# A two-hop graph kernel: the tail look-up turned round, and one operand of the second hop's vector operations kept in PSUM

## The reference

```python
def _agg(ent, rel, head, tail, etype, fc_w, fc_b):
    a_input = concatenate([ent[head], ent[tail]], -1)
    e = leaky_relu(sum((a_input @ fc_w.T + fc_b) * rel[etype], -1), 0.2)
    exp_e = exp(e - segment_max(e, head)[head])
    alpha = exp_e / segment_sum(exp_e, head)[head]
    return segment_sum(ent[tail] * alpha[:, None], head) + ent
for _ in range(2):
    ent = _agg(...)
    ent = ent / maximum(norm(ent), 1e-12)
return layernorm(x + ent)
```

## Time and profile before

| | us |
|---|---|
| median of 3 runs | 2868.09 (2825.28 to 2874.2) |
| profiled execution, its own time | 2870.03 |
| its span, first to last instruction | 2867.7 |
| busy: PE / DVE / ACT / POOL | 1218.3 / 1848.4 / 866.2 / 1805.7 |

### The profile page before, as it was taken

One profiled execution on the slowest core, in us unless ns is written; L12 is line 12 of the kernel. 1 busy time (PEld: TensorE's weight loads), 2 busy tenths in 40 slices (PEclk: granted clock), 3 DMA queues, 4 the chain that ended last, 5 costly groups with the idle time before them and its releaser, 6 DMA issues. The chain is left out here.

```text
span 2867.7 us, 22941 instructions
## 1 busy us (share of the span) xinstructions
PE 1218.3 (42%) x4597; PEld 818.2 (29%) x4597; DVE 1848.4 (64%) x3677; ACT 866.2 (30%) x1585; POOL 1805.7 (63%) x1607
## 2 busy tenths in 40 slices
PE   4688801354423544245433534444344345343300
PEld 4577701122211222123212423232223223222200
DVE  6867864286562865546655559877667667766753
ACT  2232304375453754445631212111111111111111
POOL 1000047377774777757777238877777787777776
PEclk9555555555555555555555556665655555566555
DMA  2333333254432444335433133222222222222210
GB/s 68 89 109 103 104 70 84 52 147 131 126 91 71 130 132 131 86 95 150 122 87 114 51 112 89 82 85 79 61 83 87 72 66 84 86 58 66 60 44 13
DMA packets 91815, 255.95 MB, mean 89 GB/s; under 512 B 31782, under 2 KB 39047, under 8 KB 91771
## 3 DMA queue, kind: packets, MB, share of 16 engines
q1 hardware_dynamic: 41403, 183.66, 20.8%
q0 software_dynamic: 50368, 71.78, 11.4%
HBM read 157.76 MB, written 102.23 MB: 91 GB/s over the span
## 5 line engine op out<-in xcount | busy, mean ns | idle before, releaser
L572 POOL DMA_INDIRECT area<-rows,gi x1176 | 1330.2, 1131 | 487.4 <-issue 367.7
L620 POOL DMA_INDIRECT out<-area,place x392 | 459.3, 1172 | 119.5 <-issue 119.5
L765 PE MATMUL psR<-area,row_t 128*98 128x512 f16 (+1 forms) x896 | 302.7, 504 | 454.3 <-DVE area L1191 335.9
L748 PE MATMUL psR<-area 128*128 128x392 f16 x392 | 198.5, 506 | 445.2 <-issue 406.3
L670 PE MATMUL psP<-V,vT 65*125 65x40 f32 (+1 forms) x1586 | 323.4, 393 | 86.1 <-issue 56.6
L670 PEld LDWEIGHTS psP<-V,vT 65*125 65x125 f32 (+1 forms) x1586 | 316.0, 310 | 104.7 <-issue 62.4
L765 PEld LDWEIGHTS psR<-area,row_t 128*98 128x98 f16 x896 | 141.5, 173 | 610.4 <-DVE area L1191 351.9
L908 ACT ACTIVATE area<-area 128x896 f32<-128x896 f32 x84 | 79.8, 950 | 586.2 <-DVE area L1270 433.6
L872 ACT ACTIVATE area<-iota_h,half_hi 128x392 f16<-128x392 f16 x392 | 238.9, 609 | 16.8 <-issue 15.4
L1269 DVE TENSOR_TENSOR area<-SM,rd 128x896 f32<-128x896 f32 x56 | 93.6, 1671 | 206.6 <-DMA out<-area,place 205.4
L774 PE MATMUL psT<-ones,area 98*128 98x1 f32 x700 | 152.6, 352 | 173.5 <-DVE area L1191 131.1
(11 more groups left out here) (269 smaller groups left out, 2296.4 us busy)
## 6 DMA issues: line engine op xcount, KB each, us to landing
rows<-area SPq DMA_DIRECT2D x50, 787.5 KB
area<-tail_digits SPq DMA_DIRECT2D x28, 896.0 KB
rows<-area SPq DMA_DIRECT2D x28, 735.0 KB
area<-rows SPq DMA_DIRECT2D x28, 735.0 KB
area<-rows SPq DMA_DIRECT2D x25, 787.5 KB
area<-rows,gi POOLq DMA_INDIRECT x1176
head_xs<-area SPq DMA_DIRECT2D x28, 448.0 KB
area<-head_xs SPq DMA_DIRECT2D x28, 448.0 KB
```

The lines of the kernel that those rows point to most:

```text
L572: pool.indirect_dma_start(out=to[:, b, k, 0:tab.shape[1]], out_offset=None, in_=tab, in_offset=bass.IndirectOffsetOnAxis(ap=gi[:, b, n, k: ...
L620: pool.indirect_dma_start(out=out, out_offset=bass.IndirectOffsetOnAxis(ap=place[:, b, k:k + 1].bitcast(U32), axis=0), in_=rowO[:, b, k, 0 ...
L748: te.matmul(psC, sign_lo[:, (s0 + k) % KS, :], sign_hi[:, (s0 + k) % KS, :], start=static and t0 + k == 0, stop=True, skip_group_check=True)
L765: te.matmul(psR[g % 2][0:HH, 0:w], row_t[:, n, c, :], hot_lo[:, c, 4 * g * P:4 * g * P + w], start=c == 0 and n == 0, stop=c == HB - 1 and ...
```

## The change

1. **Look-up turned round.** The tail number is split in an upper digit (tail >> 7) and a rest of 128. The digits in DRAM are now only the upper ones, broadcast to 98 partitions instead of 128. `hots` makes four one-hots of 98 x 1792. They are now the stationary operand, and the table, turned once into `row_of_hi` (8 matmuls on PE, two copies on DVE, new `turn_table`), moves: 8 matmuls of 128 columns for each of 14 columns, 112 in a chunk. `choose` is now one `scalar_tensor_tensor` with a sum over its elements for each column, which writes `tail_row` itself. L774 and `take_rows` are gone.
2. **One operand from PSUM in hop 1.** `held_*` are parts of PSUM. In hop 1 the type mask, the four operations before L1344, `ex`, `decay`, `rd`, `rs`, `mean`, `part`, `agg * rd` and the sum after L1283 read or write one of them in place of an SBUF tile. Hop 0 keeps SBUF.
3. **Drains.** In `transposes`, `products`, `count` and `look` the drain and its separate increment go; the last matmul carries the increment.

```diff
             def transposes(row, n, parts, w, tr):
...
-                    pe.drain()
-                    pe.sem_inc(tr, 1)
+                    last.then_inc(tr, 1)
...
             def products(n, parts, w, pr):
...
-                pe.drain()
-                pe.sem_inc(pr, 1)
+                last.then_inc(pr, 1)
...
             def count(j, static, half):
...
-                              start=static and t0 + k == 0, stop=True, skip_group_check=True)
-                    pe.drain()
-                    pe.sem_inc(s_cnt, 1)
+                              start=static and t0 + k == 0, stop=True, skip_group_check=True).then_inc(s_cnt, 1)
...
+            def look(j):
...
                 for g in range(4):
                     if not (isinstance(j, int) and j == 0 and g < 2):
                         pe.wait_ge(s_took, j * 4 + g - 1)
-                    for c in range(HB):
-                        for n in range(2):
-                            te.matmul(psR[g % 2][0:HH, 0:w], row_t[:, n, c, :], hot_lo[:, c, 4 * g * P:4 * g * P + w],
-                                             start=c == 0 and n == 0, stop=c == HB - 1 and n == 1)
...
+                    for k in range(4 * g, min(4 * g + 4, K)):
+                        for c in range(HB):
+                            for n in range(2):
+                                last = te.matmul(psR[g % 2][:, (k % 4) * P:(k % 4 + 1) * P], hot[0:HH, c, k * P:(k + 1) * P],
+                                                 row_of_hi[:, n, c, :], start=c == 0 and n == 0, stop=c == HB - 1 and n == 1)
+                    last.then_inc(s_look, 1)
...
             def choose(j, gs):
...
-                    ve.tensor_tensor(chosen[0:HH, of], hot_hi[0:HH, of], psR[g % 2][0:HH, 0:of.stop - of.start],
-                                     ALU.mult).then_inc(s_took, 1)
...
+                    for k in range(4 * g, min(4 * g + 4, K)):
+                        at_k = bass.ds(j * K + k, 1)
+                        last = ve.scalar_tensor_tensor(picked[:, k, :], iota_h[:, 0:P], tail_lo[:, at_k],
+                                                       psR[g % 2][:, (k % 4) * P:(k % 4 + 1) * P], ALU.is_equal, ALU.mult,
+                                                       accum_out=tail_row[:, at_k])
+                    last.then_inc(s_took, 1)
...
+                via, rd_, rs_, mean_ = (vv, rd, rs, mean) if h == 0 else (held[:, 0:K0, :], held_rd, held_rs, held_mean)
+                link(ve.tensor_tensor(via, agg, wide(rd_[:, 0:K0], K0), ALU.mult))
+                ve.tensor_tensor(vv, via, rowsH[:, :, 0:C], ALU.add).then_inc(s_sq, 1)
...
+                    link(ve.tensor_tensor(via, vv, wide(rs_[:, 0:K0], K0), ALU.mult))
+                    link(ve.tensor_tensor(vv, via, rowsX, ALU.add))
...
+                    typ_, iota_ = (typ, iota_r) if h == 0 else (held_typ, held_iota)
+                    ex_, decay_, rd_, part_ = (ex, decay, rd, part) if h == 0 else (held_ex, held_decay, held_rd, held_part)
...
                     if h == 0 and j == NCN - 1:
                         row_table()
-                        dve.wait_ge(s_map, 3)
+                        turn_table()
```

More of the change, by code:

```diff
@@ L250, in build_gnn @@
         psM = psT[:, 3, :]
-        psX = psR[0][:, 0:K]
         psC = psR[0][:, 0:HI]
         psK, psY = psR
+        flatT = psT[:, :, :].rearrange("p n x -> p (n x)")
+        held = flatT[:, 0:K * C].rearrange("p (k c) -> p k c", c=C)
+        held_A = flatT[:, 0:K * R].rearrange("p (k r) -> p k r", r=R)
+        held_typ = flatT[:, K * R:2 * K * R].rearrange("p (k r) -> p k r", r=R)
+        held_part = flatT[:, 1024 - CO - 1:1024]
+        small = flatT[:, 1024:1536]
+        held_end, small = small[:, 0:T], small[:, T:]
+        held_rd, held_rs, held_mean, held_iota, held_first, held_last = (
+            small[:, a:a + n] for a, n in ((0, K), (K, K), (2 * K, K), (3 * K, R), (3 * K + R, R), (3 * K + 2 * R, R)))
+        held_ex = psP[:, 1, 512 - 2 * K:512].rearrange("p (n k) -> p n k", n=2)
+        held_decay = psP[:, :, :].rearrange("p n x -> p (n x)")[:, 0:CO * (K + 1)].rearrange("p (c k) -> p c k", k=K + 1)
+        assert K * C <= 1024 - CO - 1 and 3 * K + 3 * R + T <= 512 and CO * (K + 1) <= 1024 - 2 * K
         s_src = sem("heads_loaded")
@@ L669, in products @@
                 for k in range(n):
-                    te.matmul(psP[0:parts, k // half, (k % half) * w:(k % half + 1) * w],
+                    last = te.matmul(psP[0:parts, k // half, (k % half) * w:(k % half + 1) * w],
                                      vT[:, k * P:k * P + parts], V[:, 0:w], start=True, stop=True)
-                pe.drain()
-                pe.sem_inc(pr, 1)
+                last.then_inc(pr, 1)
             def node_transposes(j):
@@ L721, in _ @@
             pe.wait_ge(s_dig, 1)
[L722 to L726, removed]
+            for c in range(4):
+                last = te.matmul(psR[0][0:T // 4, c * P:(c + 1) * P], digits[:, c * (T // 4):(c + 1) * (T // 4)],
+                                 ident_h[:, :], start=True, stop=True)
+            last.then_inc(s_digT, 1)
             for n in range(3):
@@ L788, in _ @@
             te.matmul(psR[1][:, 0:HI], step_p[:, :], totals[:, :], start=True, stop=True).then_inc(s_mapd, 1)
+            pe.wait_ge(s_map, 3)
+            for n in range(2):
+                for c in range(HB):
+                    last = te.matmul(psR[n][0:HH, c * P:(c + 1) * P], row_t[:, n, c, :], ident_h[:, :], start=True, stop=True)
+                last.then_inc(s_tab, 1)
             project(NCN - 1, 0)
-            pe.wait_ge(s_map, 3)
+            pe.wait_ge(s_tabc, 2)
             for n in range(3):
-                look(n, psX)
+                look(n)
                 project(NCN + n, (NCN + n) % 2)
@@ L894, in chunk @@
                     act.wait_ge(s_dl, e0 + j + 1)
-                    sc_.activation(ex[:, :, :], dl[:, :, :], ACT.Exp).then_inc(s_exp, 1)
+                    ex_, decay_ = (ex[:, :, :], decay) if h == 0 else (held_ex, held_decay)
+                    sc_.activation(ex_, dl[:, :, :], ACT.Exp).then_inc(s_exp, 1)
                     act.wait_ge(s_exp, h * NCH + j + 1)
-                    sc_.copy(decay[:, :, 1:K + 1], ex[:, 0:1, :].to_broadcast([P, CO, K])).then_inc(s_ex, 1)
+                    sc_.copy(decay_[:, :, 1:K + 1], ex_[:, 0:1, :].to_broadcast([P, CO, K])).then_inc(s_ex, 1)
                     if h == 0:
@@ L1173, in row_table, with turn_table @@
                                  ALU.mult).then_inc(s_map, 1)
+            def turn_table():
+                for n in range(2):
+                    dve.wait_ge(s_tab, n + 1)
+                    ve.tensor_copy(row_of_hi[:, n, :, :], psR[n][0:HH, :].rearrange("h (c p) -> h c p", c=HB)).then_inc(s_tabc, 1)
             def hots(j, b, i):
@@ L1273, in finish @@
                 meanwhile[0]()
[L1274 removed]
+                finish_norm(K0, root + 1, rs_)
                 if h == 0:
@@ L1294, in finish @@
                     dve.wait_ge(s_rt, root + 2)
-                    link(ve.reciprocal(rs[:, 0:K0], rs[:, 0:K0]))
-                    link(ve.tensor_tensor(rowO[:, b, 0:K0, 0:C], vv, wide(rs[:, 0:K0], K0), ALU.mult))
+                    link(ve.reciprocal(rs_[:, 0:K0], rs[:, 0:K0]))
+                    link(ve.tensor_tensor(rowO[:, b, 0:K0, 0:C], vv, wide(rs_[:, 0:K0], K0), ALU.mult))
             def nothing():
@@ L1405, in pair @@
                         q = i * 2 + b + 3
-                        chunk(i * 2 + b, b, static, True, i, look=(q, 1 - b, i + 1 + b) if h == 1 else None,
-                              taking=(q - 1,) if h == 1 and not (static and b == 0) else None)
+                        chunk(i * 2 + b, b, static, True, i, look=(q, 1 - b, i + 1 + b) if h == 1 else None)
                 link.base += link.n
```

136 lines of the change are left out of this document (54 added, 82 removed).

## The result

| on the same chip | us |
|---|---|
| before | 2859.34 (2825.28 to 2874.2) |
| changed | 3017.62 (2986.57 to 3037.79) |
| ratio | 1.060, 95% interval 1.041 to 1.078 |

The account below looks back on a forecast made before the run. Hop 1 was taken as bound by POOL's queue of indirect DMAs, hop 0 as troubled by slow spells. Terms -145 (hop 1), -69 (drains) and +12 (added in hop 0) sum to -202, giving 2666 us, range 2590 to 2750.

Parts of the forecast that it names:

- the term of hop 1: Hop 1: PSUM operands and the look-up on DVE bring POOL and DVE level at 36.2 us a chunk; -145 us (-75 to -160).
- DVE waiting in the picks for PE: Hop 1: sign named beforehand that the prediction is wrong, DVE held in the look-up's picks by PE; no size given.
- Hop 1 is POOL's queue, and a PSUM operand frees it: Hop 1: POOL works without a break; PSUM operands end 167 us of stretched gathers and scatters, POOL's period 41.7 to 35.9 us.
- PSUM doesn't free POOL: Rival, hop 1: a second SBUF reader was not what stretched gathers, so chunks stay at 41.7 us; 2811 us, chance 0.05.
- Picks: Look-up on DVE: 14 picks a chunk at 0.40 us each, 5.6 us (4.1 to 8.5), DVE's loop 35.7 us.
- Look-up on PE: 112 matmuls a chunk at 0.11 us, 12 us, or 24 if loads don't hide; either fits in 36 us.
- Drains: Removing PE's drains: nothing in hop 1, half the slow spells of hop 0 go; -69 us (-11 to -126).
- slow spells: Hop 0: PE's drains come through late, so ACT, DVE and POOL wait in turn; POOL's three rests total 89.2 us.
- spells stay: Rival, hop 0: PE's signals are late with or without a drain, -11 in place of -69; 2724 us, chance 0.21.
- Added in hop 0: Turning the table +4.3, three look-ups with more work on DVE +7, small copies before hop 1 +1; together +12 us.
- A slow spell in hop 1: Rival, hop 1: look-up matmuls up to 2.8 us more each, DVE stands in `choose`; three give 2756 us; chance 0.09.
- hop 1 had none so far with POOL just as busy: Argument against slow spells in hop 1: none had occurred there although POOL was equally busy; no size given.

Follow-up runs that it names:

- gap_h0: Kernel before without drains, plus one pause of three memsets on POOL in every second chunk of hop 0: 2826 us, ratio 1.021 on chip D.
- nodrain_only: Kernel before with its drains on PE replaced by an increment on the last matmul, nothing else: 2888 us, ratio 0.992 on chip B.
- psum_only: Kernel before with only the PSUM operands of hop 1, old look-up and drains kept: 3152 us, 1.083 on chip B; repeated on D, 2609 us, 0.941.
- psum_nodrain: Kernel before with PSUM operands and no drains, old look-up kept: 2988 us, 1.029 on chip B; repeated on E, 2601 us, 0.939.
- look_only: Changed kernel with hop-1 operands back in SBUF, drains still gone: 2949 us, 1.010 on chip B; repeated on D, 2744 us, 0.991.
- spaced_h1: Kernel before with PSUM operands and no drains, plus a one-element memset on POOL after every second indirect DMA of hop 1: 3001 us, 1.035 on chip C.

## Why the prediction was wrong, step by step

**The step that failed** is the term of hop 1, -145 us, and in it the overlap "either fits in 36": the look-up's matmuls were to take 12 us a chunk, 24 at most, hidden behind POOL and DVE. In the profiled executions on A hop 1 grew by 168 us instead (27 intervals, 1,085 to 1,253). PE was busy with the look-up's matmuls for 382.5 us and idle ahead of them, for nothing that the profile shows, for 749.9 more, together 40 us a chunk, and DVE and then POOL waited for them: the sign that the forecast itself had named, "DVE waiting in the picks for PE". The sum had no term for what an unbroken queue of POOL does to PE; it stood among the rivals. Hop 0, whose share of the forecast was -57, grew by 32. (The working's sums come out, but for one chance: what the range leaves out is 0.14, not 0.16.)

**Hop 1 is POOL's queue, and a PSUM operand frees it: right.** Gathers and scatters of hop 1 fell to 0.95 to 0.96 and 0.99 us on every chip. Where nothing holds PE up, POOL's period is 35.7 us (35.6 and 35.8 in turn) against the 35.9 of the sum, and hop 1 lost 1,085 - 933 = 152 us against 145 forecast, if before's hop 1 in its one trace is taken for that on E (gap_h0, which keeps this hop 1, took 1,083 on D). The rival "PSUM doesn't free POOL" falls, and with it, for this kernel, the statement behind it in the Trainium skill (SBUF — State Buffer, "Who interferes with whom"), that `tensor_tensor` wasn't seen to stall a GpSimd DMA: the stretched gathers went when one of its operands left SBUF. The section's other sentence, on a single SBUF input, holds there only outside the two-port modes, a condition that the forecast left out; the one-hots, with one input, did stretch a gather a little, to 1.05 us.

**Picks: priced too high.** 0.34 us each, starting 0.27 apart, with 0.08 for reading the sum, against 0.40. DVE's own loop is 33.4 to 34, not 35.7. The picks explain 1.8 of it. Two operations on the scores also fell, from 0.63 us to 0.45, with an operand in PSUM.

**Look-up on PE: right on D and E** (0.10 to 0.11 us a matmul), wrong on A by the numbers above.

**Drains: too much by most of the term.** The forecast gave half of the slow spells to them, 58 of its 69 us. nodrain_only says 0.8%, some 20 us, on B, and the spells stayed; the changed kernel had five rests of POOL over 15 us in hop 0, 120 us together, where the earlier trace rows had 89. The first and the fourth:

```profile
565.51 1.77 POOL L585 DMA_INDIRECT area<-rows,gi  x1 [36.49 <-DVE gi L1146]
...
1443.99 1.76 POOL L585 DMA_INDIRECT area<-rows,gi  x1 [25.23 <-DVE gi L1146]
```

The rival "spells stay" had it right, and the earlier trace rows were its evidence.

**Added in hop 0, +12: too high, small.** Beside it stood -11 for the sums' round trips, which go with the turned look-up too. Of the two together, +1, the runs on E make some -10 (2601 to 2592).

**The rival that came true, at 0.09, a third of it slower.** "A slow spell in hop 1" was there with its place, its 2.8 us a matmul and its end after POOL runs dry. It was thought of as a few spells of 30 us; what came was one of some 11 us in each chunk. What put its chance too low is one clause: "hop 1 had none so far with POOL just as busy". POOL's busy time was the same, but a sixth of it was gathers stretched by DVE, and the earlier trace rows and the 167 us worked out from the earlier trace rows said so. The forecast took those stretches away and kept, as evidence, a quiet that had only been seen with them. I had also noted that spells end when POOL has run dry, which points at POOL's issuing as the cause; the next question, what the change does to POOL's breaks, was not asked. That the stretches are what keeps the hold-up out of hop 1 is the likeliest reading of before beside psum_only, and of nodrain_only beside psum_nodrain on one chip, pairs which differ in the PSUM operands; it wasn't tried alone, since the seven short pauses met only a chip without the hold-up. And they can't be enough by themselves. look_only has them, mean gather 1,179 ns, and POOL still waits 50 us for indices (1980 to 2500 us). Hop 0 of before has them as well (window 420 to 1650 us), and its spells came. Before the longest rest of the earlier trace rows, two gathers in a row took 1.90 and 1.70 us, from 494.4 us on, and PE stood still until 543.2 all the same. The rows, of look_only and then of before:

```profile
L586 POOL DMA_INDIRECT area<-rows,gi x156 | 184.0, 1179 | 99.6 <-DVE gi L1148 50.4 <-issue 49.2
```
```profile
L572 POOL DMA_INDIRECT area<-rows,gi x760 | 842.3, 1108 | 337.2 <-issue 241.1 <-DVE gi L1143 96.1
```
```profile
543.22 0.50 PE L748 MATMUL psR<-area 128*128 128x392 f16 x1 [49.82 <-issue]
```

What else sets hop 1 of before apart from these two stays open.

**What no row could tell.** That the sign differs from one chip, or one time, to another: 1.060 on A and 0.936 on E for one and the same kernel. The trace before the prediction is of one execution on one chip; its late signals in hop 0, which no trace on D or E has, belonged to that chip or that time, and I read them as a mark of the kernel.

## What to carry to other kernels

If a trace shows late signals or an engine idle for "issue" while GpSimd issues DMAs back to back, then what slows GpSimd down may be part of what protects the rest: before taking it away, look whether each quiet stretch has those breaks in it. Evidence that a rival "hasn't happened so far" is worth nothing when the change removes the condition under which it was collected. Measure a change that makes GpSimd issue more densely on several chips and at several times, and always beside the kernel before on the same chip: one comparison would here have said +6% or -6% with a tight interval.

## What the runs showed of the hardware

- In the comparisons on A to C (two chips or three) PE's instructions and increments are held up while POOL issues indirect DMAs every 1.25 to 1.29 us; in the places shown of hop 1 PE or its increments came through 3.7 to 4.4 us after the last one. In those on D and E they aren't, with the same POOL durations (0.95 and 0.99 us). What differs between them isn't shown by any row. The held stretch of 2287 to 2312 us on A has packets of the one queue of POOL's DMAs and no other, and which path is blocked stays open. The Trainium skill's sentence that "PE and ACT never wait on anyone" (SBUF — State Buffer, "Who interferes with whom") is about the ports of SBUF; PE here waits while GpSimd issues, whatever the way.
- Before's own time goes with it: 2859 to 2913 us on A to C, 2767 to 2769 on D and E.
- A memset of one element between two indirect DMAs costs nothing (0.09 us inside the 0.30 between them, in spaced_h1).
- Operands that DVE or ACT write to PSUM and read back cost no time that the rows show: `XI` takes 1.74 us with `ex` in PSUM and 1.80 with it in SBUF, and `agg * rd`, whose result goes to PSUM, 1.67 us as before.
